# Moving six node pairs beside the last edge tiles, and gathers to other stages, in a four-layer graph network

## The reference

```
L0: softmax-weighted sum of edge messages per dst, then a two-layer MLP with layer norm
L1: GIN: (x + sum of x[src] per dst) through a two-layer MLP, batch norm over all nodes, residual
L2: h = x @ W_in2f; y[dst] += h[src] * filter(edge);  out = softplus(y @ W_o1) @ W_o2
L3: two SAGE layers: mean of x[src] per dst @ Wl + x @ Wr, with relu between
```

## Time and profile before

| | us |
|---|---|
| median of 3 runs | 2399.41 (2397.23 to 2402.43) |
| profiled execution, span | 2409.0 |
| stages 1 to 4 begin at about | 1107, 1310, 1710, 2068 |
| busy: TensorE, VectorE, ScalarE, POOL | 2090.2, 1990.3, 1791.3, 1507.2 |

### The profile page before, as it was taken

How to read it: one execution, slowest core, us unless ns; L and a number is a source line. 1 busy time by engine, 2 the same in 40 slices (tenths; PEclk the granted TensorE clock), 3 DMA queues, 4 the chain that set the end, 5 groups by cost and what they waited for, 6 DMA issues and landing times. The chain is left out here.

```text
span 2409.0 us, 45629 instructions
## 1 busy us (share of the span) xinstructions
PE 2090.2 (87%) x14016; PEld 1742.8 (72%) x14016; DVE 1990.3 (83%) x2945; ACT 1791.3 (74%) x3691; POOL 1507.2 (63%) x1114
## 2 busy tenths in 40 slices
PE   5999999999997899998997888888599998487564
PEld 4999999999997677775775777776466666365464
DVE  7999999999997566666996899999488888398554
ACT  4889889988896577776775788888599998276221
POOL 6888766777730434431554655777488884688787
PEclk9999999999999899998999899999899999699776
DMA  4666666555665888886885688888377775786653
GB/s 110 146 168 156 156 167 170 162 147 162 183 183 169 222 254 252 257 238 183 201 203 134 139 185 182 203 199 194 96 188 191 192 193 152 160 204 160 170 161 104
DMA packets 322547, 427.40 MB, mean 177 GB/s; under 512 B 113683, under 2 KB 169589, under 8 KB 322308
## 3 DMA queue, kind: packets, MB, share of 16 engines
q1 hardware_dynamic: 210004, 367.20, 53.6%
q0 software_dynamic: 112000, 56.93, 13.9%
q10 hardware_dynamic: 304, 0.36, 0.0%
HBM read 239.24 MB, written 185.90 MB: 176 GB/s over the span
## 5 line engine op out<-in xcount | busy, mean ns | idle before, releaser
L1782 POOL DMA_INDIRECT acc<-combined,first_ x100 | 206.9, 2069 | 186.5 <-DMA acc<-combined,first_ 77.7
L510 PE MATMUL banks<-mats,g_hT 128*125 128x256 f32 x1000 | 260.1, 383 | 0.0
L529 PE MATMUL banks<-mats,g_zT 128*125 128x128 f32 x2000 | 238.8, 273 | 0.0
L529 PEld LDWEIGHTS banks<-mats,g_zT 128*125 128x125 f32 x2000 | 228.1, 188 | 0.0
L844 POOL DMA_INDIRECT gin_xs<-x,from_ x100 | 126.5, 1265 | 162.5 <-DMA x_of_src<-gin_xs 138.5
L510 PEld LDWEIGHTS banks<-mats,g_hT 128*125 128x125 f32 x1000 | 190.2, 190 | 27.6 <-issue 0.4
L1012 DVE TENSOR_TENSOR gin_acc<-gin_acc,gin_qr 125x512 f32<-125x512 f32 x125 | 86.6, 693 | 117.1 <-ACT gin_qr L974 86.3
L590 ACT ACTIVATE g_zT<-banks,cols 128x500 f32<-128x500 f32 x250 | 178.9, 775 | 4.8 <-PE banks L518 4.8
L573 ACT ACTIVATE g_sq<-banks 125x512 f32<-125x512 f32 x250 | 144.6, 590 | 45.1 <-PE banks L510 32.2
L437 POOL DMA_INDIRECT g_xd<-in_x,idx x100 | 124.8, 1248 | 75.3 <-PE banks L544 48.4
L1837 POOL DMA_INDIRECT em_h<-h,from_ x100 | 142.4, 1424 | 43.6 <-issue 25.6
(11 more groups left out here) (408 smaller groups left out, 6613.3 us busy)
## 6 DMA issues: line engine op xcount, KB each, us to landing
acc<-g_zero SPq DMA_DIRECT2D x126, 224.0 KB
x<-g_x SPq DMA_DIRECT2D x125, 224.0 KB
g_x<-in_xT SPq DMA_DIRECT2D x100, 250.0 KB
gin_x<-x SPq DMA_DIRECT2D x50, 448.0 KB
h<-gin_hr SPq DMA_DIRECT2D x50, 448.0 KB
al_h<-h SPq DMA_DIRECT2D x38, 448.0 KB
al_x<-x SPq DMA_DIRECT2D x38, 448.0 KB
out<-al_out SPq DMA_DIRECT2D x38, 448.0 KB
```

Of the source, the lines that this page charges most:

```text
L510: m = nc.tensor.matmul(bank[0:P, 256 * j:256 * j + 256], HT[q % 2][:, c:c + P], K.W1c, start=False, stop=j == 1)
L529: m = nc.tensor.matmul(pO[q % 2][0:P, D * j:D * j + D], ZT[q % 2][:, h, P * j:P * j + P], K.W2[:, h, :], start=False, stop=j == R - 1 and ...
L1782: pool.indirect_dma_start(out=K.acc, out_offset=bass.IndirectOffsetOnAxis(ap=K.first[:, g, r:r + 1], axis=0), in_=CR[:, g, r * D:r * D + D ...
```

## The change

- 18 late pairs in place of 12, so 32 pairs in stage 2.
- Stage 4 has one list of steps per engine, over 22 steps, in which pairs and tiles alternate: tile k belongs to step `1 + k * 19 // 25`, so the steps 1 to 19 have one tile or (six of them) two. The pairs' transposes (`pA`, `pX`) have one bank each in place of two, and a tile's `turn` uses the bank of the pairs' `turn`.
- All 25 tiles have their own buffer `H`, which also takes the result; the scatters come from there.
- Before each tile's scatters POOL waits for as many stored pairs as reach up to the tile's last `dst`. The class `Allowed` counts them on VectorE at the start of the stage, and POOL loads the 25 counts into registers. SP counts `landed` up once a store has landed.
- The 16 h gathers for stage 3 stand on POOL in stage 1, ahead of the first round.
- The last 5 tiles' sum gathers (20 of the 100) stand in stage 3, ahead of its other POOL work, each tile with a semaphore for which `turn_y` waits.

```diff
-LATE = 12
+LATE = 18
+YEARLY = 20
@@ edges_first, POOL
+                for k in range(4):
+                    ins.get(pool, k)
                 for k in range(rounds):
                     past(pool, cr, k)
@@ sums_and_gather, POOL
-        for m in range(EG):
-            for r in range(R):
-                pool.indirect_dma_start(out=CR[:, m, r * D:r * D + D], out_offset=None, in_=K.acc,
-                                        in_offset=bass.IndirectOffsetOnAxis(ap=K.from_[:, m, r:r + 1], axis=0)).then_inc(got, 16)
-        for k in range(4):
-            ins.get(pool, k)
-        pool.wait_ge(got, 16 * R * EG)
+        for m in range(YEARLY):
+            ins.get_y(pool, m, got)
+        pool.wait_ge(got, 16 * R * YEARLY)
@@ class Inputs
+    def get_y(self, pool, m, landed):
+        for r in range(R):
+            pool.indirect_dma_start(out=self.CR[:, m, r * D:r * D + D], out_offset=None, in_=self.K.acc,
+                                    in_offset=bass.IndirectOffsetOnAxis(ap=self.K.from_[:, m, r:r + 1], axis=0)).then_inc(landed, 16)
@@ edges_middle
+                for k in range(YEARLY, EG):
+                    ins.get_y(pool, k, ins.y_late[k - YEARLY])
                 steps(EG, [(0, get), (5, put)])
...
                 def turn_y(k):
                     past(pe, bt, k)
+                    if k >= YEARLY:
+                        pe.wait_ge(ins.y_late[k - YEARLY], 16 * R)
@@ new
+def tiles_at(i, first=1, over=19):
+    return [k for k in range(EG) if first + k * over // EG == i]
...
+class Allowed:
+    def on_vector(self, dve):
+        nc = self.nc
+        dve.wait_ge(self.lasts_in, 16)
+        dve.wait_ge(self.edged, 1)
...
+        nc.vector.tensor_tensor(self.over[:, :, :], lasts, edges, ALU.is_ge).then_inc(self.made, 1)
+        dve.wait_ge(self.made, 1)
+        nc.vector.reduce_sum(self.sum[:, :], self.over[:, :, :], AX.X).then_inc(self.made, 1)
+        dve.wait_ge(self.made, 2)
+        nc.vector.tensor_scalar(self.need[:, :], self.sum[:, :], 1.0, None, ALU.add).then_inc(self.needed, 1)
+    def values(self, pool):
+        pool.wait_ge(self.needed, 1)
+        return [pool.value_load(self.need[0:1, k:k + 1], min_val=1, max_val=LATE + 1) for k in range(EG)]
@@ edges_last
-        n = LateNodes(nc, K, out, "lt", ctx, NG // 2 - LATE, LATE, (K.ps[0], K.ps[1:3], K.ps[3:5], K.ps[5], K.pairs[3]))
+        n = LateNodes(nc, K, out, "lt", ctx, NG // 2 - LATE, LATE, (K.ps[0], K.ps[1:2], K.ps[3:4], K.ps[5], K.pairs[3]))
-        pT, pC = K.ps[1:3], K.ps[3:5]
+        pT, pC = K.ps[0], [K.ps[2], K.ps[4]]
@@ edges_last, POOL
-                for k in range(EG):
-                    get(k)
-                n.all_stored(pool)
-                for k in range(EG):
-                    put(k)
+                need = allowed.values(pool)
+                for k in range(EG):
                     past(pool, done, k)
+                    pool.wait_ge(landed, need[k])
@@ edges_last, SP
+                for i in range(STEPS + 3):
                     n.load(sp, i)
+                    if i == 0:
+                        allowed.load(sp)
                     if i >= 3:
                         n.load_was(sp, i - 3)
                     if i >= 5:
                         n.store(sp, i - 5)
-                for k in range(EG):
-                    load(k)
+                    if i >= 2:
+                        each(load)(i - 1)
+                    tell(i - 6)
@@ edges_last, TensorE
-                nodes_on_pe(n, pe)
-                steps(EG, [(0, turn), (0, second)])
+                steps(STEPS, [(2, on(n.turn_x3, pe, 0)), (0, lambda i: turn_pair(i, 0)), (2, on(n.turn_x3, pe, 1)),
+                              (0, lambda i: turn_pair(i, 1)), (2, on(n.hidden, pe, 0)), (0, on(n.turn_back, pe, 0)), (0, turn),
+                              (2, on(n.hidden, pe, 1)), (0, on(n.turn_back, pe, 1)), (2, on(n.second, pe, 0)), (2, on(n.second, pe, 1)),
+                              (0, each(second))])
@@ edges_last, ScalarE
+                steps(STEPS, [(1, on(n.exp_a, act)), (2, on(n.copy_x3, act, 0)), (0, on(n.relu_b, act, 0)), (2, on(n.copy_x3, act, 1)),
+                              (3, on(n.log_c, act)), (3, on(n.exp_c, act)), (0, on(n.relu_b, act, 1)), (0, each(copy)),
+                              (2, on(n.relu_h, act, 0)), (1, on(n.square_b, act)), (2, on(n.relu_h, act, 1)), (1, on(n.log_b, act)),
+                              (1, on(n.exp_b, act)), (0, on(n.square_a, act)),
+                              (1, each(lambda k: norm.square(act, k, flat(H[k]), c))), (1, each(root)), (2, on(n.square_c, act)),
+                              (0, on(n.log_a, act))])
@@ edges_last, VectorE
+                allowed.on_vector(dve)
+                steps(STEPS, [(1, on(n.apply_a, dve)), (1, on(n.add_alone, dve)), (3, on(n.apply_c, dve)), (0, on(n.residual, dve, 0)),
+                              (0, each(sums)), (1, on(n.reduce_b, dve)), (0, on(n.residual, dve, 1)), (0, each(average)),
+                              (1, on(n.apply_b, dve)), (1, each(residual)), (0, on(n.reduce_a, dve)), (3, on(n.which, dve)),
+                              (1, each(norm.reduce_of(dve))), (3, on(n.blend, dve)), (1, each(apply)), (2, on(n.reduce_c, dve))])
```

More of the change, by code:

```diff
@@ L1505, in _, with edges_first @@
                               (2, on(n.reduce_c, dve))])
-def edges_first(nc, K, CR, rounds):
+def edges_first(nc, K, CR, rounds, ins):
     name, last = "ef", EG - 1
@@ L1815, in __init__, with tiles, loads @@
     def __init__(self, nc, K, CR, ctx):
[L1816 to L1822, removed]
+        self.nc, self.K, self.CR, self.ctx = nc, K, CR, ctx
+        self.H = self.tiles("h", 4)
+        self.got = K.lasting("em_got", 4)
+    def tiles(self, n, k):
+        return [self.ctx.enter_context(self.nc.sbuf_tensor(f"em_{n}{i}", [P, R, D], F32)) for i in range(k)]
+    def loads(self):
+        self.X, self.XD, self.YD = self.tiles("x", 2), self.tiles("xd", 3), self.tiles("yd", 3)
+        self.IV = [self.ctx.enter_context(self.nc.sbuf_tensor(f"em_iv{i}", [128, G], F32)) for i in range(3)]
+        self.xin, self.din = self.K.lasting("em_xin", 2), self.K.lasting("em_din", 3)
+        self.y_late = self.K.lasting("em_y_late", EG - YEARLY)
     def Y(self, k):
@@ L2199, in _, with each, run_all, turned_before @@
                            (0, soft_d), (1, nc_.reduce_of(dve)), (0, nb.reduce_of(dve)), (0, join_d), (1, rows_hd)])
+def tiles_at(i, first=1, over=19):
+    return [k for k in range(EG) if first + k * over // EG == i]
+def each(stage):
+    def run_all(i):
+        for k in tiles_at(i):
+            stage(k)
+    return run_all
+def turned_before(i):
+    return sum(len(tiles_at(j)) for j in range(i))
+class Allowed:
+    def __init__(self, nc, K, ctx):
+        self.nc, self.K = nc, K
+        self.lasts = ctx.enter_context(nc.sbuf_tensor("el_lasts", [1, EG], I32))
+        self.edges = ctx.enter_context(nc.sbuf_tensor("el_edges", [1, LATE], F32))
+        self.over = ctx.enter_context(nc.sbuf_tensor("el_over", [1, EG, LATE], F32))
+        self.sum = ctx.enter_context(nc.sbuf_tensor("el_over_sum", [1, EG], F32))
+        self.need = ctx.enter_context(nc.sbuf_tensor("el_need", [1, EG], I32))
+        self.lasts_in, self.edged, self.made, self.needed = [K.sem(f"el_{n}") for n in ("lasts_in", "edged", "made", "needed")]
+    def load(self, sp):
+        sp.dma_start(self.lasts[:, :], self.K.I["dlast"]).then_inc(self.lasts_in, 16)
+    def on_gpsimd(self, pool):
+        self.nc.gpsimd.iota(self.edges[:, :], pattern=[[2 * G, LATE]], base=N - 2 * G * LATE, channel_multiplier=0,
+                            allow_small_or_imprecise_dtypes=True).then_inc(self.edged, 1)
+    def on_vector(self, dve):
+        nc = self.nc
+        dve.wait_ge(self.lasts_in, 16)
+        dve.wait_ge(self.edged, 1)
+        lasts = self.lasts[:, :].rearrange("p (g o) -> p g o", o=1).to_broadcast([1, EG, LATE])
+        edges = self.edges[:, :].rearrange("p (o l) -> p o l", o=1).to_broadcast([1, EG, LATE])
+        nc.vector.tensor_tensor(self.over[:, :, :], lasts, edges, ALU.is_ge).then_inc(self.made, 1)
[6 more added lines that the diff above has]
+        return [pool.value_load(self.need[0:1, k:k + 1], min_val=1, max_val=LATE + 1) for k in range(EG)]
 def edges_last(nc, K, out):
@@ L2297, in copy, with root @@
                     past(act, scan, k - 2)
-                    nc.scalar.activation(HT[k % 2][:, :], pT[k % 2][:, 0:G], ACT.Copy).then_inc(ht, 1)
+                    nc.scalar.activation(HT[k % 2][:, :], pT[:, 0:G], ACT.Copy).then_inc(ht, 1)
+                def root(k):
+                    norm.log(act, k)
+                    norm.exp(act, k, done)
                 nc.scalar.preload_act_table_set("natural_log_exp_and_others")
-                nodes_on_act(n, act)
-                steps(EG, [(1, lambda k: norm.square(act, k, flat(C[k % 3]), c)), (0, copy), (1, norm.log_of(act)),
-                           (1, lambda k: norm.exp(act, k, done))])
```

(13 more changed lines are left out.)

61 lines of the change are left out of this document (34 added, 27 removed).

## The result

The changed kernel takes 2379.15 us (median) beside 2402.43 us of before on the same chip: ratio 0.990, 95% interval 0.987 to 0.992. Timed a second time, again beside the kernel before, it took 2374.13 beside 2405.77: 0.987, 0.984 to 0.989. By the ratios it is 25 to 32 us faster, where 40 were forecast; both medians lie in the range that was named (2339 to 2384). (Ratios leave out single executions that were disturbed.)

A forecast was written before the change was run, and what follows sets the result against it. VectorE was taken to set the pace wherever pairs run, and POOL's scatters behind scatters to end the last stage. Terms -56 + 0 + 1 + 15 = -40 took 2399.4 to 2359 us, range 2339 to 2384.

The forecast's parts named there:

- Stages 1 and 2, -56 forecast: Stage of pairs alone: VectorE's and POOL's queues both shorten by 56 us; -56, bounds -50 to -62.
- h gathers ahead, 0 forecast: Before the rounds: sixteen h gathers fit into POOL's 28.3 us wait and cost nothing.
- Twenty sum gathers behind, +1 forecast: Middle stage: 30.2 us of gathers mostly covered by POOL's 27.1 us of waits; +1, bounds 0 and +9.
- Stage 4, +15 forecast: Last stage: POOL's 100 gathers, then 100 scatters at 1.77 us beside VectorE's work, end at 2418; +15 us.
- Small things: Last stage: tile loads issued behind the blend, about 10 us ahead of use; nothing charged, up to 2.5 us a step.
- VectorE has about 1 us a step to lose: Last stage: with 16.6 us steps, tile 24 may be scattered 15 us before POOL comes to it.
- rival 2: Last stage: step chain sets the end, 2.5 us more in 17 steps; stage +42, 2386 us; chance 0.20.
- the main forecast: Last stage: POOL sets the end; total 2359 us, 2345 to 2366; chance 0.52.
- the register loads, 3 us: Last stage, between gathers and scatters: 25 loads take 3 us, at most 38; over 10 us would show it wrong.
- Rival 3: Early stages: h gathers delay the rounds, up to 24 us, half made up; -40 + 12, 2371 us; chance 0.05.
- Rival 4: Last stage: VectorE's two-SBUF-input operations block POOL, slot 3.06 us; stage +106, 2450 us, slower; chance 0.06.
- Rival 1: Last stage: scatters stay cheap at 1.57 us, tile chain ends at 2403; stage 0, 2344 us; chance 0.17.

The follow-up runs named there:

- experiment 3: Kernel before with only the two moves on GpSimd's queue (h gathers ahead, 20 late sum gathers), 12 late pairs, old stage 4: 2396.5 us, 0.995.
- experiment 2: Changed kernel with the 16 h gathers put back behind the sum gathers of stage 2: 2400.61 us, 0.996 of before.
- experiment 6: Tile loads issued first, 32 late sum gathers in place of 20: 2366.07 us (0.983) with 18 late pairs, 2354.42 us (0.980) with 19.
- With the loads first: Changed kernel, SyncE issuing a step's tile loads ahead of the pair's old-row load and store: 2359.91 us, repeated 2358.54 us, both 0.980 of before.
- experiments 3 and 4: 3 has its own line; 4 is the changed kernel with the old stage 4 (all 18 late pairs, then tiles): 2412.24 us, 1.003 of before.

## Why the prediction was right in the two early stages and wrong in the last

*Stages 1 and 2, -56 forecast.* The five profiles whose stages 1 and 2 are those of the changed kernel have a mean of 549.6 us, the two of before 607.9: -58; single profiles lie between 547 and 553, and at 603 and 613. The step was right, and so was its reason: VectorE and GpSimd ended close together, and GpSimd's shortening alone brought little (experiment 3). After the change GpSimd ends the stage, in those five profiles 8 to 18 us behind VectorE's last pair.

*h gathers ahead, 0 forecast.* Right; shown by experiment 2, which brings 23 us back.

*Twenty sum gathers behind, +1 forecast.* Right: stage 3 is 359.4 us in the mean of the same five profiles, 359.1 in the two of before. Its cover is shown by experiment 6: at 32 gathers it is gone.

*Stage 4, +15 forecast; measured +24 and +27.* This is where the prediction failed, and the step is the one under "Small things": the tile's three loads, issued behind the blend, for which nothing was charged, with 2.5 us a step as the bound. They cost 1 us a step (18.0 and 18.1 against 16.9 and 17.1), 15.6 us in all. The step was reckoned with a load that lands in 5.55 us and is used 10 us later. In the trace above the issue comes 4.1 us after the blend's end (2208.01 - 2203.90), behind the pair's two transfers and the tile's other two, and the landing another 6.92 us later, by when VectorE has waited 1.7 us. The rest, "VectorE has about 1 us a step to lose", was right: the loads took just that, the steps are another 0.3 to 0.5 us longer than reckoned, and they took over from GpSimd. The forecast's conclusion that GpSimd sets the end fell with it, and rival 2, which had been given 0.20, is what happened, at 2374 to 2379 us instead of 2386. The range held because it took most of rival 2 in, not because the main forecast (GpSimd sets the end, 2345 to 2366 us) came true.

With the loads out of the way, GpSimd's terms can be checked. First gather to last gather's end was forecast at 173 us and took 170 and 167; the register loads, 3 us, and added none (0.31 us from the last gather to the first scatter, as between any two). They were not cheap: the 25 took 15.6 us of GpSimd's sequencer in the changed kernel (2160.6 to 2176.2; the view of their line is in the last section), more than the 10 us named as a sign of being wrong, but it ran them while the engine still worked on gathers issued before; the scatters, 173 us, and took 173.1 and 173.3. That last sum hit, its price did not: a slot without a rest was 1.66 and 1.60 us, not 1.77, and 10 and 17 us of rests and waits made up the difference. Stage 4 is then +9 (mean 342.1 against 332.8), 6 less than forecast because of the first two terms, and GpSimd and the steps end it level.

*The sum.* -58.2 + 0.3 + 25.5 = -32 us from the profiles of the changed kernel (mean stage 4 358.3 us), timed -25 and -32. With the loads first -58.2 + 0.3 + 9.3 = -49, timed -47 and -48.

*The rivals.* Rival 3 fell by experiment 2. Rival 4 needs 2.2 us a slot; in the changed kernel a gather's was 1.67 and a scatter's without a wait 1.61. Rival 1 had the slot nearly right, and missed because the steps set the end. The Trainium skill, SBUF — State Buffer, "Who interferes with whom", states that a VectorE instruction with two SBUF inputs contends with GpSimd's reads. The prediction found that its rows agree in direction only, because it read the mean of a slot, 1.79 us beside pairs; beside pairs and tiles it was 1.60 to 1.66 us a scatter, against 1.49 beside nothing. Single transfers show it in full. Timelines of GpSimd and of VectorE in the pair loop of before:

```profile
2160.78 2.16 POOL L2230 DMA_INDIRECT el_h<-h,of_h  x1 [0.30 <-issue]
2163.24 1.96 POOL L2230 DMA_INDIRECT el_h<-h,of_h  x1 [0.30 <-issue]
2165.51 1.21 POOL L2230 DMA_INDIRECT el_h<-h,of_h  x1 [0.31 <-issue]
```

```profile
2160.60 1.29 DVE L1449 COPY_PREDICATED lt_out<-lt_set,lt_was 125x1024 f32<-125x1024 int32 x1
...
2162.91 1.21 DVE L1388 TENSOR_TENSOR lt_b<-lt_a,lt_na_r 125x1024 f32<-125x1024 f32 x1
```

The first two gathers start while VectorE runs an operation on two SBUF tiles, and each ends 1.0 to 1.1 us after that operation; the third and the three behind it, which do not, take 1.21 us. In stage 4 of the two profiles of before, every transfer that started with more than 0.15 us of such an operation left (88) ended 1.0 to 1.1 us after it, and none of the other 312 took more than 1.25 us. So GpSimd is held, for what is left of the operation, and only by one that already runs when the transfer starts. That makes the mean: (4 x 1.51 + 2.46 + 2.26)/6 = 1.79 us a slot. Rival 4 charged every such operation in full and fell for that reason, not because nothing is held.

## What to carry to other kernels

When two loops are interleaved, follow each queue that both now share, SyncE's too: a load that was early in a list of its own becomes late behind the other loop's transfers (here the old rows and the store), which wait for that loop's last operation. Ask of each load what stands ahead of it in its queue and what that waits for; here one reordering gave 16 us without a buffer more. And where two engines end a stage level, shortening one shows little until the other is shortened as well (11 of 58 us here), and the next move lands on whatever cover is already used up.

## What the runs showed of the hardware that was not expected

TensorE's granted clock is lower in the interleaved stage. In the pair loop of before it was 1.00; in the same window of the changed kernel (busy us of TensorE, its weight loads, VectorE, ScalarE and GpSimd, then the granted clock, DMA share and GB/s):

```profile
2120.00:2206.00 86.00, 62.28 (x428) 53.44 (x429) 73.39 (x85) 47.67 (x94) 69.99 (x53) 0.92 0.87 208
```

that is, part of it at 1.2 GHz. TensorE was busy 62.3 of these 86 us, against 69.7 before, and over stage 4 it shows waits of up to 3.8 us for ScalarE's copies. Eight matmuls of L1282 take 1.91 us at the lower level (granted clock 0.50 from 2227.0 to 2229.5) and 1.04 at the higher (1.00 from 2231.0 to 2240.0), as its timeline shows 5 us apart:

```profile
2227.35 1.91 PE L1282 MATMUL banks<-cm,lt_bT 128*125 128x128 f32 x8
2232.11 1.04 PE L1282 MATMUL banks<-cm,lt_bT 128*125 128x128 f32 x8
```

What this adds to a step was not measured by itself.

In the new stage 4, GpSimd rests 2.8 to 6.9 us ahead of the 40th and of the 79th scatter, in the middle of a tile's four, where the program has no wait. With the loads first:

```profile
2260.29 1.19 POOL L2305 DMA_INDIRECT out<-el_h,to_d  x1 [6.91 <-issue]
```

In both profiles of before, and in experiments 3 and 4 with the old stage 4, the same row of scatters has no rest at all; what makes these was not tried.

A register load took 0.6 us of GpSimd's sequencer, with the two operations that follow each (25 in 15.6 us), and the 25, followed by waits on their values, left no gap between the last gather and the first scatter. Their line in the changed kernel:

```profile
L2267 POOLq TENSOR_LOAD <-el_need x25: 282/289/1554, 2160.6 to 2175.7; - x25
L2267 POOLq SEQ_ASSERT  x25: 18/18/32, 2161.3 to 2176.2; - x25
```

(ns min/median/max, then the starts of the first and the last.)
